# The row table of a mixture-of-experts layer: placing products in halves, one comparison for the slot one-hots, multiplies on GpSimd, and logits by token

## The reference, cut to what matters

```python
logits = xt @ gate_w.T                          # 8192 x 15
scores = softmax(logits, axis=-1)
topk_w, topk_idx = top_k(scores, 3)
topk_w = topk_w / (sum(topk_w, -1, keepdims=True) + 1e-20)
...                                              # each token's three experts, weighted
hs = xt @ s_fc1_w.T + s_fc1_b                   # the shared expert, width 512
as_ = gelu(hs[..., 512:]) * hs[..., :512] * s_geglu_mult
ys = as_ @ s_fc2_w.T + s_fc2_b
```

## Time and profile before

| | |
|---|---|
| median of 3 runs | 1864.28 us (1864.2 to 1865.15) |
| the profiled execution, its own time | 1861.96 us |
| its span in the trace | 1860.1 us |
| mean granted TensorE clock | 0.929 of 2.4 GHz |
| routing stage in the trace | about 608 to 1062 us |
| slots 0 to 39 | 636.2 to 1025.9 us |

### The profile page before, as it was taken

How to read it: one execution, slowest core, us unless ns; L and a number is a source line. 1 busy time by engine, 2 the same in 40 slices (tenths; PEclk the granted TensorE clock), 3 DMA queues, 4 the chain that set the end, 5 groups by cost and what they waited for, 6 DMA issues and landing times. The chain is left out here.

```text
span 1860.1 us, 25518 instructions
## 1 busy us (share of the span) xinstructions
PE 1545.6 (83%) x6044; PEld 956.1 (51%) x6044; DVE 1171.2 (63%) x2485; ACT 872.6 (47%) x1490; POOL 934.9 (50%) x818
## 2 busy tenths in 40 slices
PE   6883666666776578878788599999999999997997
PEld 3332444444544245545455456666666666664555
DVE  5656999999998455455555644444444444443598
ACT  6887898998896222122211133343333433332210
POOL 6887888888884210110000056666666666663000
PEclk9996888899889699889989899999999999998999
DMA  4323233333321533332102222222222222223895
GB/s 146 139 98 136 102 103 113 125 125 111 114 93 61 197 116 110 110 111 89 46 35 109 104 80 88 86 88 88 88 85 88 88 88 88 86 87 133 330 339 215
DMA packets 68444, 215.78 MB, mean 116 GB/s; under 512 B 13680, under 2 KB 14704, under 8 KB 68208
## 3 DMA queue, kind: packets, MB, share of 16 engines
q1 hardware_dynamic: 41520, 132.71, 19.9%
q0 software_dynamic: 21696, 60.84, 9.9%
q10 hardware_dynamic: 5120, 20.86, 3.2%
HBM read 147.78 MB, written 66.58 MB: 115 GB/s over the span
## 5 line engine op out<-in xcount | busy, mean ns | idle before, releaser
L1866 PE MATMUL bank<-arena_dt,xgT 128*128 x832 | 393.4, 595 | 0.3 <-issue 0.3
L738 POOL TENSOR_TENSOR state<-arena_x,b_all 128x1024 f32<-128x1024 f32 x128 | 301.7, 2369 | 67.1 <-issue 64.5
L762 PE MATMUL bank<-ident,state 128*128 128x128 f32 x1024 | 200.4, 330 | 153.6 <-ACT scaled L675 72.6
L1958 DVE TENSOR_TENSOR hid<-bank,arena_x 128x512 f32<-128x512 f32 x208 | 143.9, 692 | 251.0 <-PE bank L1866 251.0
L817 DVE TENSOR_TENSOR_SCAN state<-bank,state 128x1024 f32<-128x1024 f32 x128 | 292.2, 2284 | 5.0 <-POOL state L738 4.9
L1827 POOL DMA_INDIRECT choice_out<-ye,ids x208 | 205.4, 988 | 162.4 <-DVE ye L1972 159.1
L762 PEld LDWEIGHTS bank<-ident,state 128*128 128x128 f32 x1024 | 156.0, 211 | 203.4 <-DVE state L817 112.8
L1818 POOL DMA_INDIRECT xg<-x_norm,tokens x208 | 202.5, 973 | 71.8 <-issue 60.9
L1933 ACT ACTIVATE gluT<-bank 128x256 f32<-128x256 f32 x208 | 80.0, 385 | 322.0 <-PE bank L1875 320.5
L1883 PE MATMUL bank<-arena_x,gluT 128*128 x832 | 213.9, 380 | 0.0
L1866 PEld LDWEIGHTS bank<-arena_dt,xgT 128*128 128x128 f32 x832 | 142.5, 191 | 100.8 <-issue 100.7
(11 more groups left out here) (212 smaller groups left out, 2531.0 us busy)
## 6 DMA issues: line engine op xcount, KB each, us to landing
b_all<-bc_rows SPq DMA_DIRECT2D x64, 512.0 KB, 3.6
arena_x<-choice_out SPq DMA_DIRECT2D x16, 1536.0 KB, 10.2
xin<-in_x SPq DMA_DIRECT2D x16, 512.0 KB, 3.5
x_skip<-xin SPq DMA_DIRECT2D x16, 512.0 KB, 2.6
y_acc<-x_skip SPq DMA_DIRECT2D x8, 1024.0 KB, 6.7
x_mid<-y_acc SPq DMA_DIRECT2D x8, 1024.0 KB, 6.4
arena_x<-x_mid SPq DMA_DIRECT2D x16, 512.0 KB, 5.2
x_norm<-arena_x SPq DMA_DIRECT2D x16, 512.0 KB
```

The lines of the kernel that those rows point to most:

```text
L738: pool.tensor_tensor(state[j % STATES][:, :, here], gT[:, :, b, here], b_all[j % BUFS][:, here].unsqueeze(1).to_broadcast([P, KD, TH]), AL ...
L762: last = pe.transpose(bank[:, TURN + (BY_PE * j + q) % 2, i * D + k * P:i * D + (k + 1) * P], state[j % STATES][:, k, t // GT * CH + t % G ...
L1866: last = pe.matmul(bank[:, 2 + s, :], xgT[s][:, k, :], w1[:, k, ds(e_no * (2 * F), 2 * F)], start=(k == 0), stop=(k == KD - 1))
L1958: dve.tensor_tensor(hid[s][:], bank[:, 2 + s, :], b1[:, ds(e_no * (2 * F), 2 * F)], ALU.add).then_inc(hid_made, 1)
```

## The change

The routing step `logits` turns its product round: now the 128 tokens of a tile are stationary and the 15 gate columns move, so the logits come out with tokens on partitions, as `three_best` wants them. `turn_logits`, `copy_logits` and the buffer `logitT` go. In `hots`, six one-hots are made by one comparison of 768 columns, and GpSimd multiplies the choice numbers in, in place; two semaphores (`slots_hot`, `numbers_in`) join the two. `place` runs one half at a time, at the end of its slot instead of ahead of `fc1`: half 0 in slot +7, half 1 in slot +8. On DVE `keep_out` moves from ahead of `glu` to just ahead of `hots`, and when two halves fall in one slot the older group's is made first.

```diff
@@ GpSimd
+                    rstds(3)
                     for g in range(GROUPS):
-                        if g + 3 < GROUPS:
-                            rstds(g + 3)
+                        if g + 4 < GROUPS:
+                            rstds(g + 4)
+                        for h in range(2):
+                            pool.wait_ge(slots_hot, 2 * g + h + 1)
+                            pool.tensor_tensor(
+                                slot_hot[h], slot_hot[h],
+                                choice_all[:, ds(g * GK + h * HK, HK)].unsqueeze(2).to_broadcast([P, HK, P]), ALU.mult)\
+                                .then_inc(numbers_in, 1)
@@ TensorE
                     def logits(g):
-                        for k in range(KD):
-                            last = pe.matmul(bank[0:E, 3, :], gate[:, k, :], xnT[g % 4][:, k, :], start=(k == 0),
-                                             stop=(k == KD - 1))
+                        for i in range(GT):
+                            for k in range(KD):
+                                last = pe.matmul(bank[:, 3, i * (E + 1):i * (E + 1) + E], xnT[g % 4][:, k, i * P:(i + 1) * P],
+                                                 gate[:, k, :], start=(k == 0), stop=(k == KD - 1))
-                    def turn_logits(g):
...
-                    def place(g, n_ranked):
+                    def place(g, h, n_ranked):
+                        if h == 0:
+                            wait(pe, rank_read, n_ranked)
+                            wait(pe, out_kept, g)
+                        pe.wait_ge(hots_made, 2 * g + h + 1)
+                        pe.wait_ge(numbers_in, 2 * g + h + 1)
...
-                        for g in routed_at(q - 2):
-                            turn_logits(g)
-                        for g in routed_at(q - 8):
-                            place(g, n_ranked)
-                            n_placed += 1
...
                         if j >= 1 and i < 2:
                             fc2(j - 1, i)
+                        for h in (1, 0):
+                            for g in routed_at(q - 7 - h):
+                                place(g, h, n_ranked)
+                                n_placed += h
@@ ScalarE
-                    def copy_logits(g):
...
-                        for g in routed_at(q - 1):
-                            copy_logits(g)
@@ VectorE
                     def hots(g, h):
-                        for m in range(HK):
-                            at = h * HK + m
-                            dve.tensor_scalar(slot_hot[h][:, m, :], number[:, 0:P], slot_block[g % 2][:, 0, at:at + 1],
-                                              choice_all[:, g * GK + at:g * GK + at + 1], ALU.is_equal, ALU.mult)
+                        dve.tensor_tensor(
+                            slot_hot[h], number[:, 0:P].unsqueeze(1).to_broadcast([P, HK, P]),
+                            slot_block[g % 2][:, 0, h * HK:(h + 1) * HK].unsqueeze(2).to_broadcast([P, HK, P]), ALU.is_equal)\
+                            .then_inc(slots_hot, 1)
...
-                        for g in routed_at(q - 8):
-                            keep_out(g)
...
                         if i == 3 and 0 <= j < G1:
                             add_bias(j)
-                        for h in range(2):
+                        for g in routed_at(q - 8):
+                            keep_out(g)
+                        for h in (1, 0):
                             for g in routed_at(q - 6 - h):
                                 hots(g, h)
```

More of the change, by code:

```diff
@@ L1173, in model_kernel @@
             spare = late + 6 * GD
-            logitT = arena_x[0:E, spare:spare + GN]
-            spare += GN
             CHOSEN = GT * TOPK * E
@@ L1250, in model_kernel @@
                 "xnT_made")]
-            logits_done, logitT_made, logits_turned, logits_kept, best_made, at_made, index_made = [sem(n) for n in (
-                "logits_done", "logitT_made", "logits_turned", "logits_kept", "best_made", "at_made", "index_made")]
+            logits_done, logits_kept, best_made, at_made, index_made = [sem(n) for n in (
+                "logits_done", "logits_kept", "best_made", "at_made", "index_made")]
             chosen_made, taken_made, seen_made, ranked, rank_read, row_step, rows_made = [sem(n) for n in (
@@ L1258, in model_kernel @@
             table_step, shift_made, exp_made = [sem(n) for n in ("table_step", "shift_made", "exp_made")]
-            hots_made, hots_read, out_kept = [sem(n) for n in (
-                "hots_made", "hots_read", "out_kept")]
+            slots_hot, numbers_in, hots_made, hots_read, out_kept = [sem(n) for n in (
+                "slots_hot", "numbers_in", "hots_made", "hots_read", "out_kept")]
             blocks_made, blocks_spread, tiles_hot, tile_hot_read, ids_kept = [sem(n) for n in (
@@ L1411, in rank @@
                                   start=False, stop=True).then_inc(ranked, 1)
-                    def place(g, n_ranked):
-                        wait(pe, rank_read, n_ranked)
-                        wait(pe, out_kept, g)
-                        for h in range(2):
-                            pe.wait_ge(hots_made, 2 * g + h + 1)
-                            for m in range(HK):
-                                last = pe.matmul(bank[0:COLS, 7, P:2 * P], column_hot[h][:, m, :], slot_hot[h][:, m, :],
-                                                 start=(h == 0 and m == 0), stop=(h == 1 and m == HK - 1))
-                            last.then_inc(hots_read, 1)
+                    def place(g, h, n_ranked):
[4 more added lines that the diff above has]
+                        pe.wait_ge(numbers_in, 2 * g + h + 1)
+                        for m in range(HK):
+                            last = pe.matmul(bank[0:COLS, 7, P:2 * P], column_hot[h][:, m, :], slot_hot[h][:, m, :],
+                                             start=(h == 0 and m == 0), stop=(h == 1 and m == HK - 1))
+                        last.then_inc(hots_read, 1)
                     def fc1(q):
@@ L1503, in copy_xnT @@
                         act.activation(xnT[g % 4][:], bank[:, 4:6, :], ACT.Copy).then_inc(xnT_made, 1)
-                    def copy_logits(g):
-                        act.wait_ge(logits_done, g + 1)
-                        wait(act, logits_turned, g)
-                        act.activation(logitT, bank[0:E, 3, :], ACT.Copy).then_inc(logitT_made, 1)
                     def gelu(q):
@@ L1546, in _ @@
                         if q == turn_slot(GROUPS - 1) + 5:
-                            act.wait_ge(logits_turned, GROUPS)
+                            act.wait_ge(logits_done, GROUPS)
                             act.wait_ge(ranked, GROUPS)
@@ L1574, in three_best @@
                     def three_best(g):
-                        dve.wait_ge(logits_turned, g + 1)
+                        dve.wait_ge(logits_done, g + 1)
                         here = slice(g * GT, (g + 1) * GT)
```

## The result

The changed kernel takes **1777.07 us** (median of 4 runs, 1776.22 to 1781.92), against 1864.24 for the kernel before in the same session: a ratio of 0.9537, 95% interval 0.9519 to 0.9554. The profiled execution has a span of 1775.4 us (before 1860.1).

What follows compares the result with a forecast made beforehand. PE was taken to bound the routing slots, stopped by DVE's one-hots. Gone 86.3 less new 25 gave loop 61.3; with front 5 and tail 5, 71 us: 1793 from the profiled 1861.96 plus 2.3 for the median; range 1772 to 1828.

Steps and rivals of the forecast that it cites:

- What bounds the kernel: Routing stage, slots 0 to 39: PE sets each slot's end and is stopped by DVE's one-hots about once per group.
- The waits and the slow running that go: In the loop: 56.2 us of PE waits for `column_hot`, and 22 of 30 us lost at 1.2 GHz, would go.
- The waits that come: New PE waits in the loop: 15 us for half 1, 1 for half 0, 4.6 behind `scale_w2`, 4.4 for `rank`.
- `scale_w2`: Behind a half's comparisons in slots 25, 28, 31, it holds GpSimd off; two lack `fc2` to cover it: 4.6 us.
- waits of 2.4 and 1.5: PE's remaining wait for half 1's one-hots: 2.4 us for an odd group, 1.5 for an even one.
- thin cover: Half 0 of an odd group: a chain of 4.22 us hidden behind 4.68 on PE, a cover of 0.46 us.
- The clock: 8 us of slow running left out of 30: three for the first slots, five behind the new waits.
- `rank`, `normalise`, logits: PE in the loop: `rank` waits add 4.4 us, covered `normalise` waits save 4.1, 16 logits products take 1.88 per group.
- Front and tail: Before the first `fc1`, 5 us saved by an earlier `three_best`; after slot 39, 5 us from one-hot waits and slow running.
- The clock falling all the same: Rival, chance 0.13: some 18 short waits in the loop each bring slow running, 38 us instead of 8; time 1823.
- GpSimd and DVE in each other's way: Rival, chance 0.10: multiplies hold up two-operand DVE instructions by up to 1.82 us; half 1 waits 35 us; time 1824.
- GpSimd as the bound: Rival, chance 0.05: 768-column multiplies far slower, so every half waits; the gain is gone at 4.8 us a multiply.

## Why the prediction was right, and where its sizes were off

*What bounds the kernel.* Right. PE waits for the one-hots in slots 0 to 39, and moving `place` alone takes 78.5 us off the loop.

*The waits and the slow running that go.* Right. The 56.2 us went, and with them most of the 30 at 1.2 GHz.

*The waits that come* were put at 15 for half 1, 1 for half 0 and 4.6 behind `scale_w2`: 20.6 us. They measured 9.0 + 2.1 = 11.1. The term that was mis-sized is the chain of half 1, in "I let GpSimd begin only when L1642 has ended", with 1.82 for the multiply: 0.95 + 0.90 + 1.82 = 3.67 from the start of the slot comparison to the end of the multiply. On the trace that is 852.71 - 849.63 = 3.08. That the two engines take turns was nearly right: of the 0.74 us that the multiply lies under L1634 it loses 0.60. What was too long is the multiply's own 1.82, by 0.35; the other 0.24 are small overlaps from step to step. With 0.6 less, the prediction's own waits of 2.4 and 1.5 become 1.8 and 0.9, and PE's waits are just that: 1.82 at 687.34 (and 1.84 once), 0.92 at 713.45 (and twice more). The sixth is the 2.63 shown above, 1.8 like the others of its kind and 0.8 behind `scale_w2`. By the prediction's counts (4 and 3.5 halves) that is 4 x 1.8 + 3.5 x 0.9 = 10.4; the trace has 8.2 in 6 and the 0.8. Half 0 waits nowhere for its one-hots: its thin cover became 1.1 us.

*`scale_w2`* was put at 4.6 and cost some 2.9 (2.11 and the 0.8), by a path that the prediction did not have. It does not hold GpSimd off: the multiply at 838.76 takes its usual 2.07. It is held up itself, and half 0 waits for `rows` behind it. Nor is it two of the three slots that PE can't cover, but one: behind those of slots 28 and 31 PE runs `fc2` (869.48, 892.28) and does not wait for them.

*The clock.* 8 us of slow running were left in the forecast; a clock of 0.99 over 311.8 leaves some 3. That is luck in part. The 3.38 that the prediction leaned on the earlier trace rows was one of several: in the kernel before, waits of 3.37 at 780.45 and 3.38 at 941.55 were followed by 12 products of 2.85 and 2.91 us, the slow rate. And in the run with the column one-hots first a wait of 2.05 was followed by slow running. The two kinds of waits, 9.5 less, and the clock, 5 less, are 14.5 of the 16.6 by which the loop beat its forecast. The other 2.1 are not shown; the logits may hold them, since alone they took 5.9 off PE's busy time where 4 were forecast.

*`rank`, `normalise`, logits.* 4.4, 4.1 and 1.88 forecast; 4.3 in 8, 4.1 in 4, and 1.86 for the 16 products measured. The experiment with the logits alone bears out that they save little in the loop.

*Front and tail.* 5 and 5 forecast, 5.1 and 5.4 measured. The front is the part that the logits own (19.10 with them alone): `three_best` no longer waits for the copy and the small transposes. The tail is the part of `place` (18.20 with it alone); GpSimd's multiply lengthens it, since without it the tail is 16.85.

*The rivals.* The clock falling all the same: it did not here, but the run with the column one-hots first shows that it can, for 8 us. GpSimd and DVE in each other's way: the mechanism is there, and its place is the one that was named. DVE instructions with two SBUF operands that start under a multiply are held up: `scale_w2` in three of four by 1.27 us, `add_bias` twice from 1.21 to 1.83, a small product in the tail from 0.35 to 1.62. In the slots it cost PE little, and not 35 us. The wait of 2.11 is 1.51 in the runs without GpSimd, where `scale_w2` keeps its 2.02, so 0.6 of it is this rival's, and some part of the 0.8 behind it. What stands behind `hots` on DVE is often `glu`, which reads one operand from PSUM and was not held: it kept its 0.74 to 0.75 us under 12 multiplies. The Trainium skill (Perfetto Trace Analysis, Optimizing Scalar/DVE Operations) says that moving work between these two engines might not help; the runs agree in the outcome, 1773.96 us without GpSimd (0.9517) against 1777.07 with it (0.9537). GpSimd as the bound was excluded by the multiply's length: 2.07, far from the 4.8 at which the gain would have gone.

*What the forecast did not say.* It costed the change as one whole. Part by part, the move of `place` is nearly all of it, loop and tail, the logits are the front's 5 us, and the one-hots with GpSimd, the most intricate part, give nothing and are slower by themselves.

## What to carry to other kernels

When a matrix engine waits for a producer once in each period, first move its consumer to where that wait is covered by the period's own work; here that gave 78 us of the loop with no instruction made faster. Work taken off an engine that is not the bound is worth nothing unless it shortens the chain that the bound waits for: DVE lost 15 us of load, the chain grew by a GpSimd step, and alone the edit was slower. Then look at what is queued ahead of the late producer and is wanted by nobody soon: putting the norm of a later group behind the one-hots took another 8 us off the loop without GpSimd (311.7 to 303.4) and 10 with it (311.8 to 301.6), for a move of three lines.

## What the runs showed of the hardware that was not expected

- A GpSimd multiply of 128x768 with its second operand repeated along the innermost axis took 1.47 us while DVE ran the small operations of `three_best`, less than the line through 626 ns for 206 columns and 2364 ns for 1024 gives (1.82). Started 0.16 us into a DVE comparison it took 2.07.
- Between a GpSimd multiply and a DVE instruction with two SBUF operands, the one that started second lost nearly the whole overlap, all but some 0.14 us, on either side. The multiply lay 0.74 us under L1634 and lost 0.60, and L1634 kept its 0.90. `scale_w2` lay 1.42 under a multiply and lost 1.27, `add_bias` 0.75 and 0.62, and the multiply kept its 2.07. In the run with the column one-hots first a multiply started 0.16 into `scale_w2`, lay 1.86 under it and took 3.18 for its 1.47, and `scale_w2` kept its 2.02.
- Waits of 2.05 and 2.06 us in one execution were followed by 1.2 GHz once and by 2.4 GHz once. The length of the wait before it does not settle the clock; what does was not found here.
